# The Newton step of the local layers' inverse norms: three VectorE instructions or four GpSimd instructions

## The reference, cut to what matters

```python
def l2norm(t):
    return t / jnp.maximum(jnp.linalg.norm(t, axis=-1, keepdims=True), 1e-12)
...
q = l2norm(q) * qs
k = l2norm(k) * ksc
q = q * cos * scale + rotate_half(q) * sin * scale
k = k * cos * inv + rotate_half(k) * sin * inv
out = local_attention(q, k, v)
...
mu = x.mean(-1, keepdims=True)
var = ((x - mu) ** 2).mean(-1, keepdims=True)
xn = (x - mu) / jnp.sqrt(var + 1e-05) * g + bln
```

## Time and profile before

| | |
|---|---|
| median of 3 runs | 3802.07 us |
| lowest, highest | 3801.65, 3807.49 us |
| span of the profiled execution | 3799.8 us |
| median less that span | 2.3 us |
| PE, DVE, ACT, POOL busy | 83%, 71%, 59%, 38% |
| local stage, from about 1890 us to the end | 1910 us |
| DVE busy in 2500 to 2700 us | 156.8 of 200 us |
| POOL busy in 2500 to 2700 us | 121.9 of 200 us |
| granted PE clock in 2500 to 2700 us | 1.00 |

### The profile page before, as it was taken

How to read it: one execution, slowest core, us unless ns; L and a number is a source line. 1 busy time by engine, 2 the same in 40 slices (tenths; PEclk the granted TensorE clock), 3 DMA queues, 4 the chain that set the end, 5 groups by cost and what they waited for, 6 DMA issues and landing times.

```text
span 3799.8 us, 102343 instructions
## 1 busy us (share of the span) xinstructions
PE 3156.4 (83%) x41325; PEld 2042.2 (54%) x41325; DVE 2683.2 (71%) x7106; ACT 2234.7 (59%) x5603; POOL 1457.8 (38%) x1443
## 2 busy tenths in 40 slices
PE   7878876727767879877679999999999999999997
PEld 5544544612323546545446666666666666666665
DVE  6466656537896554579787878777777777777773
ACT  4234442426554332268757777777777777777775
POOL 0110011336572000000066665656665666565651
PEclk9989987968897989989899999999999999999997
DMA  1000002710000000000001011101110201111110
GB/s 54 1 5 1 2 12 54 228 65 0 0 1 5 2 1 1 14 17 1 30 21 32 22 32 51 32 22 42 41 32 22 61 22 29 54 29 24 28 26 22
DMA packets 50453, 108.05 MB, mean 28 GB/s; under 512 B 7376, under 2 KB 17488, under 8 KB 48192
## 3 DMA queue, kind: packets, MB, share of 16 engines
q1 hardware_dynamic: 47456, 96.33, 9.3%
q0 software_dynamic: 2528, 5.18, 0.7%
HBM read 52.27 MB, written 5.18 MB: 15 GB/s over the span
## 4 chain that ended last, share of the span: by engine, by line
PE 45%; DVE 23%; ACT 13%; issue 6%; POOL 3%; DMA 1%; POOLq 0%; SPq 0%; DVEq 0%; ACTq 0%
PE psum L3240 5%; PE psum L3297 5%; PE psum L403 5%; PE psum L3280 4%; PE psum L1218 4%; PE psum L3190 4%; PE psum L408 3%; PE psum L2071 3%; DVE scratch L3452 2%; DVE xnT L3606 2%; PE psum L1272 2%; DVE xnT L3489 2%; ACT L3356 1%; PE psum L3265 1%; DVE scratch L3454 1%
## 5 line engine op out<-in xcount | busy, mean ns | idle before, releaser
L3646 POOL TENSOR_TENSOR scratch<-scratch 128x512 f32<-128x512 f32 x384 | 488.4, 1272 | 409.1 <-DVE scratch L3455 409.1
L408 PEld LDWEIGHTS psum<-table,scratch 128*128 128x128 f32 (+1 forms) x2284 | 283.1, 145 | 294.2 <-issue 234.1
L3297 PE MATMUL psum<-weights,scratch 128*128 128x512 f32 x768 | 413.6, 621 | 15.0 <-ACT y L3392 14.5
L408 PE MATMUL psum<-table,scratch 128*128 128x128 f32 (+1 forms) x2284 | 370.1, 283 | 44.5 <-DVE scratch L2772 11.8
L3659 POOL TENSOR_TENSOR scratch<-scratch,xnT 128x512 f32<-128x512 f32 x384 | 402.2, 1047 | 0.0
L3452 DVE TENSOR_TENSOR scratch<-psum,xnT 128x512 f32<-128x512 f32 x384 | 264.3, 688 | 146.0 <-PE psum L3297 139.4
L3426 ACT COPY scratch<-psum 128x512 f32<-128x512 f32 x384 | 225.8, 588 | 155.7 <-PE psum L408 149.8
L3392 ACT ACTIVATE y<-psum 128x512 f32<-128x512 f32 x384 | 230.9, 601 | 104.9 <-DVE scratch L3455 91.9
L3606 DVE TENSOR_REDUCE xnT<-y 128x8 f32<-128x512 f32 x384 | 253.9, 661 | 1.4
L1218 PE MATMUL psum<-scratch 32*128 32x256 f32 (+1 forms) x2560 | 180.2, 394 | 72.2 <-DVE weights L1479 22.2
L3581 DVE TENSOR_REDUCE scratch<-psum 128x4 f32<-128x256 f32 x384 | 161.1, 420 | 72.6 <-PE psum L3265 71.2
(11 more groups left out here) (550 smaller groups left out, 7632.6 us busy)
## 6 DMA issues: line engine op xcount, KB each, us to landing
scratch<-scratch SPq DMA_DIRECT2D x96, 256.0 KB
scratch<-experts_dram SPq DMA_DIRECT2D x47, 384.0 KB
scratch<-scratch SPq DMA_DIRECT2D x96, 128.0 KB
weights<-layer_dram SPq DMA_DIRECT2D x6, 1357.0 KB, 9.8
weights<-layer_dram SPq DMA_DIRECT2D x6, 1356.5 KB, 7.2
scratch<-scratch SPq DMA_DIRECT2D x96, 64.0 KB
weights<-gqa_dram SPq DMA_DIRECT2D x2, 1738.5 KB, 8.8
results_dram<-scratch SPq DMA_DIRECT2D x11, 256.0 KB
```

The costliest lines, as they stand in the source:

```text
L408: return self.nc.tensor.transpose(out, src, self.c("ident")[0:k, 0:k])
L3297: mm(raw_bank(a), window(m)[:, i * P:i * P + P], weight(m, "wqkv")[:, at:at + 512], start=True, stop=True).then_inc(S("rows_made").up(), 1)
L3646: gtt(out, out, sines, ALU.add).then_inc(S("rope_sum").up(), 1)
```

## The change

DVE no longer makes the Newton step. POOL makes it in the same step of the loop, after the division of the probabilities (L3652) and in front of the scaling (L3659). GpSimd gets four instructions in place of the three: two products, one multiply and add with constants, and a product, each settled before the next. The semaphore `inverse` is raised by POOL, and its waiters stay as they are.

```diff
--- before.py
+++ after.py
@@ -3480,17 +3480,6 @@
             dve.wait_ge(S("var_out"), m - 3)
         ts(x, x, 1e-24, None, ALU.max).then_inc(S("clamped").up(), 1)
 
-    def dve_exact(s):
-        m, half, first, last = root_of(s)
-        x, y, t = (lengths[m % 2][:, j, first:last] for j in range(3))
-        dve.wait_ge(S("guessed"), roots.index((m, half)))
-        tt(t, x, y, ALU.mult).then_inc(dve.link(), 1)
-        dve.settle()
-        stt(t, t, -0.5, y, ALU.mult, ALU.mult).then_inc(dve.link(), 1)
-        dve.settle()
-        stt(y, t, 1.5, y, ALU.add, ALU.mult).then_inc(S("inverse").up(), 1)
-
-
     def numbers_of(k):
         return numbers[:, 0:6 * k].rearrange("p (t s) -> p t s", s=6), numbers[:, 32:32 + 4 * k].rearrange("p (r t) -> p r t", r=4)
 
@@ -3549,8 +3538,6 @@
                 dve.wait_ge(S("turned"), t)
                 dve.wait_ge(S("valued"), t - 2)
                 nc.vector.tensor_copy(turned[t % 2], TURNED.rearrange("p (j n) -> p j n", j=2)).then_inc(S("copied_dve").up(), 1)
-            if root_of(s - 2):
-                dve_exact(s - 2)
             f = unit_at(s, 2, 1)
             if f is not None:
                 dve.wait_ge(S("ones"), f)
@@ -3620,6 +3607,19 @@
             last = gtt(rope[l % 2][:, j], two(c(tab)), weight(l * BATCH, sc).unsqueeze(1).broadcast_to([P, 2, LDIM]), ALU.mult)
             last.then_inc(S("tables").up() if j == 3 else pool.link(), 1)
 
+    def pool_exact(s):
+
+        m, half, first, last = root_of(s)
+        x, y, t = (lengths[m % 2][:, j, first:last] for j in range(3))
+        pool.wait_ge(S("guessed"), roots.index((m, half)))
+        gtt(t, x, y, ALU.mult).then_inc(pool.link(), 1)
+        pool.settle()
+        gtt(t, t, y, ALU.mult).then_inc(pool.link(), 1)
+        pool.settle()
+        nc.gpsimd.tensor_scalar(t, t, -0.5, 1.5, ALU.mult, ALU.add).then_inc(pool.link(), 1)
+        pool.settle()
+        gtt(y, y, t, ALU.mult).then_inc(S("inverse").up(), 1)
+
     def pool_program():
 
         pool.wait_ge(S("xn_dve"), M.by_dve * GROUPS - 1)
@@ -3650,6 +3650,8 @@
                 pool.wait_ge(S("exped"), t)
                 pool.wait_ge(S("turned"), t - 2)
                 gtt(probs[t % 2], E[t % 2], over_keys(small[t % 4][:, 1, :]), ALU.mult).then_inc(S("divided_pool").up(), 1)
+            if root_of(s - 2):
+                pool_exact(s - 2)
             k = s + 6
             if 0 <= k < PARTS:
                 m, q = divmod(k, 8)
```

## The result

The changed kernel takes 3849.74 us (median of 4 runs, 3840.17 to 3852.05) against 3801.86 us for the kernel before in the same session: a ratio of 1.0124 with a 95% interval of 1.0108 to 1.0141. The forecast was 3842, slower. The change is small, 1.24%, but the interval leaves 1 out.

A forecast was written before the change was run, and what follows sets the result against it. Bound by a loop of waits, no engine full. The wait at L3415 (+44.6), fill (-3) and drain (-1.5) give +40 us on the 3799.8 span; with the median 2.3 above the span, 3842 us, range 3820 to 3874.

The forecast's parts named there:

- Part 4: At p=0, ACT's L3415 waits for POOL's inverse and starts 0.97 us later; 46 units pay, +44.6 us.
- Part 3: On POOL at p=0, behind the wait for the reciprocal, the four instructions with settles take 1.04 us.
- rival A: Small GpSimd instructions have a floor: four dependent ones cost near 1.74 us; time 3860 to 3874; chance 0.13.
- Parts 1 and 2: 1.63 us leave DVE: worth 0.19 us a unit at p=0, nothing at p=4, where DVE waits for PE.
- Rival B: At p=4, freed DVE time shortens the chain and outweighs the wait at L3415; with all of it 3767; chance 0.07.
- Rival C: Work piled up behind L3415 fills later waits, so the unit stays at 38.18; time 3798; chance 0.03.
- Part 6: The two ends of the stage: the fill gives back 3 us, the drain 1.5 us.

The follow-up runs named there:

- half-and-half pair: Against the kernel before, the Newton step on POOL only at p=4 (3796.05 us, ratio 0.9996) or only at p=0 (3843.55 us, ratio 1.0121).
- two placements without a wait: Changed kernel with POOL's Newton step in front of the division L3652 (3786.11 us) or one loop step earlier, behind the scaling (3780.53 us).
- three instructions: Changed kernel without the multiply-add of POOL's Newton step: 3833.23 us.
- DVE, behind the reciprocal: Kernel before with the Newton step still on DVE, moved behind the reciprocal L3589 in the same step: 3882.26 us.
- five: Changed kernel with the first product of POOL's Newton step issued twice: 3910.80 us.
- six: Changed kernel with the first product of POOL's Newton step issued three times: 3928.48 us.

## Why the prediction was right

- **The wait at L3415** (Part 4) is what the time went to. The forecast was 0.97 us a unit and 46 units; measured were 1.06 us and 47 waits, 45 of them of 1.1 us. The half-and-half pair and the two placements without a wait show it as the cause.
- **The price of the four** (Part 3) was 1.04 us; L3415 starts 1.25 after the first product, with 1.12 forecast hand-over included. The products take 0.247 at 34 columns, where I had 0.195; the multiply-add takes 0.228 (0.26), the settles 0.08 (0.065), the hand-over to ACT 0.03 (0.08). This is the mis-sized term. I had drawn a line through 128 and 512 columns; in the changed kernel 2 columns cost 0.196 and 34 cost 0.247, so there is a floor that the line misses. Of rival A a small part was true. With L3568 starting 0.03 us sooner than assumed, 0.13 more here makes the 0.09 to 0.10 us by which the unit was forecast too short.
- **The relief of DVE** (Parts 1 and 2): 0.19 at p=0 and nothing at p=4 was forecast; 0.18 (without the step) and 0 (only p=4 moved: 38.17) were measured. Rival B fell.
- **Starts at p=0**: L3568 now starts 0.14 after the end of the scores (0.17 assumed), and L3652 0.08 after the reciprocal, as assumed.
- **Rival C** fell: the unit grew by all of the delay, and nothing made it good.
- **The ends** (Part 6): from the first DVE rotation (1893.7 before, 1894.8 after) to the first L3415 it took 110.5 us before and 108.6 after. That L3415 already carries the wait, so the fill gave back about 2.9, with 3 forecast. The drain gave 0.2 instead of 1.5: from the third last unit's L3415 to the end 78.4 us before and 78.2 after.
- **The sum.** 45 x 1.06 = 47.7 of the difference of spans of 49.6. The first rotation started 1.1 later in this execution, in stages that were not changed, the fill to the first L3415 took 1.9 less, the drain 0.2 less. The other 2.9 lie between 3651 and 3771 us, where the changed kernel has one unit of 42.76 us and one of 37.56, against 40.02 and 35.26 before. In both of these the granted clock dips:

```profile
3651.70:3694.46 42.76, 37.98 (x655) 25.38 (x652) 31.05 (x85) 30.57 (x85) 25.30 (x33) 0.96 0.11 24
...
3733.70:3771.30 37.60, 32.59 (x636) 23.49 (x636) 15.73 (x51) 25.86 (x78) 15.17 (x25) 0.91 0.11 26
```

The columns are as above; 0.96 and 0.91 are the clocks of the two units, and the unit between has 1.00. Before, the answering stretches had 1.00. The forecast had no term for this. The kernel with only the p=0 step on POOL settles it: its clock is 1.00 in both of these units, and they take 41.07 and 36.32 us, just 1.05 and 1.06 more than before. So the dips cost 1.69 and 1.24 us, which is the 2.9. They need not come from the new wait. With the Newton step in front of the division nothing waits there, and the same unit has a dip at the same place, some 14 us in, and takes 41.66 us, against 39.97 at 1.00 with the step one loop step earlier.

The time forecast is closer than its terms. On spans 40 us were forecast and 49.6 came: 4.1 from the unit (46 times 0.09), 1.3 from the drain, 2.9 from the clock, 1.1 from stages that were not changed. All four err the same way. By luck the medians hide some 2 us of this: the forecast took the median as 2.3 above the profiled span, as in the kernel before, and the changed kernel's is 0.3 above.

The weighing of the rule in the Trainium skill, "GPSIMD Engine Reference", section on engine selection, came out between: by twice DVE's 0.18 a product would take 0.36, by my line 0.195; it took 0.247, that is 1.34 times the 0.184 of DVE's L3487 at this width.

## What to carry to other kernels

Before moving work to an idle engine, find the first waiter of its result and the last wait that stands in front of the work in the new queue: here that was the reciprocal, and the work landed behind the very thing that ran ahead of its waiter. The same four instructions, 0.6 us up in POOL's order or one step earlier, turn +1.2% into -0.4%. A long instruction on the chain need not be worth its length: taking 1.63 us off DVE at p=0 gave 0.18 us, because behind DVE another wait ended 0.18 us sooner: ACT's, for PE's values.

## What was not expected of the hardware

- In these kernels a DVE instruction with two SBUF inputs is held until a POOL instruction that runs beside it ends, each time anew: 1.27 us beside the rotation's sum (97 of the 102 L3489 of the kernel before run beside a POOL instruction, with a median of 1.27), and behind the reciprocal two in a row, 0.63 and 0.97 us. With no POOL instruction beside them, those of 34 columns took 0.16 (L3487) to 0.20 us (L3491).
- Small GpSimd products have a floor: in the changed kernel 0.196 us at 2 columns, 0.247 at 34, 0.408 at 128.
- A wait of PE that grows by 0.3 us can cost 1.7, but the length of the wait does not tell when. Of the first 42 units of each run, those in which the clock fell behind PE's wait in front of L3206 are:

| kernel | PE idle there, us | units with a fall |
|---|---|---|
| before | 0.41 | 0 |
| three instructions | 1.15 | 3 |
| DVE, behind the reciprocal | 1.35 | 17 |
| changed | 1.47 | 0 |
| five | 1.78 | 41 |
| six | 2.12 | 40 |

The kernel with 1.47 us had no fall, and two with shorter waits had some. What sets it apart from them is open.
